# Attention of a Perceiver block: where the weights are turned, which of them are multiplied in fp32, and how far ahead the scores run

## The reference

```python
# 128 queries; 2048 context rows and the 128 latents as keys and values; DM 512
# 32 query heads of 128, 4 key/value heads, 8 query heads to each
q = (latents @ Wq).reshape(b, q_len, 4, 8, 128)
k = (hidden_states @ Wk).reshape(b, kv_len, 4, 128)      # kv_len 2176
v = (hidden_states @ Wv).reshape(b, kv_len, 4, 128)
scores = einsum('bqhgd,bkhd->bhgqk', q, k) * 128 ** -0.5
attn = softmax(scores)
out = einsum('bhgqk,bkhd->bqhgd', attn, v)
return out.reshape(b, q_len, 4096) @ Wo
```

## Time and profile before

| | |
|---|---|
| time, median of 3 runs | 661.22 us (659.51 to 661.26) |
| profiled execution | 660.41 us; span of its instructions 657.9 us |
| busy | PE 638.9 us (97%), PEld 546.6 (83%), DVE 451.4 (69%), ACT 362.3 (55%), POOL 203.9 (31%) |
| granted TensorE clock | 1.00 |
| DMA | 104.80 MB, mean 159 GB/s |
| attention loop | from about 119 us to 388 us of the span |

### The profile page before, as it was taken

One profiled execution on the slowest core, in us unless ns is written; L12 is line 12 of the kernel. 1 busy time (PEld: TensorE's weight loads), 2 busy tenths in 40 slices (PEclk: granted clock), 3 DMA queues, 4 the chain that ended last, 5 costly groups with the idle time before them and its releaser, 6 DMA issues.

```text
span 657.9 us, 12479 instructions
## 1 busy us (share of the span) xinstructions
PE 638.9 (97%) x4212; PEld 546.6 (83%) x4212; DVE 451.4 (69%) x1056; ACT 362.3 (55%) x711; POOL 203.9 (31%) x150
## 2 busy tenths in 40 slices
PE   7999999999999999999999999998999999999998
PEld 6888888898899989998999879987788797797473
DVE  3533143787788878787888665979975856758873
ACT  3413115777787778767877744767354444447210
POOL 0000000644674478447755454003320220200000
PEclk9999999999999999999999999999999999999999
DMA  7611002226254442625242656674657658597600
GB/s 254 273 64 62 4 0 69 78 69 196 73 153 121 135 137 73 195 67 193 60 130 67 229 236 166 246 281 151 237 214 269 249 201 298 212 350 294 250 1 16
DMA packets 27224, 104.80 MB, mean 159 GB/s; under 512 B 7424, under 2 KB 7808, under 8 KB 17584
## 3 DMA queue, kind: packets, MB, share of 16 engines
q1 hardware_dynamic: 26608, 103.23, 45.9%
q10 hardware_dynamic: 576, 1.05, 0.5%
HBM read 86.30 MB, written 0.26 MB: 132 GB/s over the span
## 4 chain that ended last, share of the span: by engine, by line
PE 86%; DVE 4%; POOL 4%; ACT 3%; issue 1%; DMA 1%; SPq 0%; ACTq 0%; DVEq 0%
PE ps L1467 19%; PE ps L1225 14%; PE ps L1226 14%; PE ps L1227 14%; PE ps L1507 8%; PE ps L1358 4%; PE ps L1302 3%; POOL pt_lo L430 3%; PE ps L1496 2%; PE ps L1617 2%; PE ps L1580 1%; DVE acc L1056 1%; DMA ring<-wk_dram 1%; POOL k_lo L430 1%; PE ps L1487 1%
## 5 line engine op out<-in xcount | busy, mean ns | idle before, releaser
L1467 PEld LDWEIGHTS ps<-norm_t,ring 128*128 128x128 f32 x1152 | 131.5, 192 | 4.8 <-issue 4.1
L1467 PE MATMUL ps<-norm_t,ring 128*128 128x128 f32 x1152 | 133.1, 276 | 0.0
L1056 DVE SCALAR_TENSOR_TENSOR acc<-raw,cw,acc 128x127 f32<-128x127 f32 (+2 forms) x240 | 85.9, 432 | 23.1 <-ACT acc L710 22.2
L430 POOL TENSOR_TENSOR pt_lo<-far_t,pt_hi 128x512 fp32r<-128x512 f32 (+1 forms) x75 | 87.3, 1183 | 37.9 <-ACT pt_hi L524 37.7
L1225 PE MATMUL ps<-pt_hi,v_hi 128*128 128x256 f32 x272 | 84.6, 311 | 3.0 <-POOL pt_lo L430 2.7
L524 ACT ACTIVATE pt_hi<-ps 128x512 fp32r<-128x512 f32 (+1 forms) x69 | 41.0, 596 | 67.1 <-PE ps L1358 67.0
L1227 PE MATMUL ps<-pt_lo,v_hi 128*128 128x256 f32 x272 | 76.6, 282 | 0.0
L1226 PE MATMUL ps<-pt_hi,v_lo 128*128 128x256 f32 x272 | 76.5, 281 | 0.0
L915 DVE TENSOR_SCALAR_CACHE_REDUCE prob_near<-ps 128x512 f32<-128x512 f32 x64 | 44.2, 691 | 24.4 <-PE ps L1227 22.6
L817 DVE TENSOR_TENSOR pt_lo<-ps,pt_hi 128x512 fp32r<-128x512 f32 (+1 forms) x69 | 47.4, 688 | 18.9 <-ACT pt_hi L524 17.6
L499 POOL TENSOR_SCALAR_AFFINE_SELECT at_hi<-a_hi 128x2048 fp32r<-128x2048 f32 x8 | 17.0, 2130 | 136.6 <-PE ps L1479 125.5
(11 more groups left out here) (205 smaller groups left out, 1311.0 us busy)
## 6 DMA issues: line engine op xcount, KB each, us to landing
ring<-w_in_dram SPq DMA_DIRECT2D x36, 1024.0 KB, 4.9
far_t<-blocks_t SPq DMA_DIRECT2D x240, 72.0 KB, 2.0
ring<-w_out_dram SPq DMA_DIRECT2D x16, 1024.0 KB, 4.9
ring<-wq_dram SPq DMA_DIRECT2D x8, 1024.0 KB, 5.1
ring<-wo_dram SPq DMA_DIRECT2D x8, 1024.0 KB, 6.9
w_sb<-w_dram SPq DMA_DIRECT2D x4, 896.0 KB, 9.1
ring<-ctx_t_dram SPq DMA_DIRECT2D x3, 1024.0 KB, 6.8
ring<-w_dram SPq DMA_DIRECT2D x3, 1024.0 KB, 8.6
```

The source lines that it names most:

```text
L430: sub = lambda dst, a, hi: pool.tensor_tensor(dst, a, hi, ALU.subtract)
L1056: ins = nc.vector.scalar_tensor_tensor(a[:, i, back:], r[:, i, 0:T - back], cw[:, bass.ds(tile + i, 1), 3 - back:4 - back].rearrange("p a ...
L1467: ins = mm(ps[:, bank, t * T:t * T + T], w[:, t, c, :], norm_t[:, c, :], start=(c == 0), stop=(c == NC - 1))
```

## The change

Only tiles 0 and 1 are still turned on PE, for every pair. Tiles 2 to 16 are turned on DVE in place (`p_far`, which replaces `prob_far` and `blocks_t`; two buffers now, one of them over ring slots 2 and 3), and moved by 16 DMAs of 32 partitions by 3840 B (2304 B before). Tiles 13 to 16 are multiplied in plain fp32 from `far_t` and `v_all` and need no split; the other values are split as before. The five score chunks have 256, 512, 512, 512 and 384 keys, and lie in PSUM as three pieces (256, 1024, 896 keys) in pairs of banks; DVE copies and ACT takes exp by piece. Step n makes the scores of pair n+2 (chunks 1 to 9) and chunk 0 of pair n+3, and the queries of pair n+3. Wq and Wo come in halves of 0.5 MB, one for each pair. The last two steps, 14 and 15, have their lo halves made by DVE; the last pair's moves are issued half on SP, half on ACT. The unchanged rest of the kernel begins with the norm behind the last output.

```diff
-PIECES = ((0, 512), (512, 1024), (1024, 1536), (1536, 2176))
+EDGES = (0, 256, 768, 1280, 1792, 2176)
+NEAR = 256
+PIECES = ((0, 256), (256, 1280), (1280, 2176))
+PIECE_OF = (0, 1, 1, 2, 2)
+FP32_TILES = {1: (13, 14), 2: (15, 16)}
+V_TILES = 13
+V_PARTS = ((0, 2), (2, 8), (8, 13))
+FAR_UNITS = UNITS - 3
+SCORES_LEAD = {1: (2,)}
+SCORES_AT = {0: (1,), 2: (3, 4), 3: (5, 6), 4: (7, 8), 5: (9,)}
...
+def tiles_of(u):
+    if u == 0:
+        return 0, 1
+    if u in FP32_TILES:
+        return FP32_TILES[u]
+    return tuple(t for t in (2 * u - 4, 2 * u - 3) if t < V_TILES)
...
@ SP
+            for n in range(LAST_PAIR):
+                if n + 4 <= LAST_PAIR:
+                    wq_load(n + 4)
+                moves(n + 1)
+                wo_load(n + 1)
...
+            sp.wait_ge(moved[0], MOVED * PAIRS_ALL // 2)
...
@ POOL: one pass of its loop
+                far_split(n, 3)
+                far_split(n, 4)
+                if n:
+                    wo_split(n - 1)
+                far_split(n, 5)
...
+                far_split(n, 6)
...
+                far_split(n, 7)
...
+                far_split(n, 8)
...
+            wo_split(LAST_PAIR - 2)
+            wo_split(LAST_PAIR - 1)
+            wo_split(LAST_PAIR, last_wo_lo, last_wo_hi)
@ ACT: attn_step(n, kv, p)
+                if not begin:
+                    act.wait_ge(pv_ps, 9 * n)
+                    act.wait_ge(wo_ps, 2 * n - 2)
+                    o_split(1 - b)
+                if not (isinstance(n, int) and n == LAST_PAIR):
+                    soft_exp(n + 1, 1 - b, 1, 0)
+                act.wait_ge(pv_ps, 9 * n + 1)
+                act.wait_ge(moved[b], MOVED * (2 * kv + p // 2 + 1))
+                far_split(b, 3)
+                far_split(b, 4)
+                far_split(b, 5)
...
+                if isinstance(n, int) and n == LAST_PAIR - 1:
+                    act.wait_ge(turned, 2 * LAST_PAIR + 2)
+                    act.wait_ge(pfl_ok, FAR_UNITS * (LAST_PAIR - 1))
+                    far_moves(act, LAST_PAIR, range(2, 4))
+                if not begin:
+                    wo_split(n - 1, 2 * kv + (p - 1) // 2, (p - 1) % 2)
+                if isinstance(n, int) and n == LAST_PAIR:
+                    wo_split(n, 2 * kv + 1, 1, last_wo_hi)
+                act.wait_ge(pv_ps, 9 * n + 4)
+                far_split(b, 6)
+                if not tail:
+                    soft_exp(n + 2, b, 0, 1)
...
+                act.wait_ge(pv_ps, 9 * n + 5)
+                far_split(b, 7)
+                if not tail:
+                    soft_exp(n + 2, b, 0, 2)
+                    soft_exp(n + 2, b, 0, 0)
...
+                act.wait_ge(pv_ps, 9 * n + 6)
+                far_split(b, 8)
...
+                    soft_exp(n + 2, b, 1, 1)
+                if ask:
+                    q_split(n + 3, 1 - b, 6 + (1 - b))
+                if not (isinstance(n, int) and n == LAST_PAIR):
+                    act.wait_ge(pv_ps, 9 * n + 7)
+                    near_split(n + 1)
...
+                    soft_exp(n + 2, b, 1, 2)
@ DVE: turn_far and attn_step(n, kv, p)
+                blocks = p_far[b][:, :, :, h, :]
+                nc.vector.transpose(blocks, blocks).then_inc(turned, 1)
...
+                if not end:
+                    turn_far(n + 1, 1 - b, 1)
+                if not tail:
+                    scores_out(n + 2, b, 0, 1, sent)
+                if not (isinstance(n, int) and n < 1):
+                    o_split(n - 1, 1 - b)
+                if not (isinstance(n, int) and n < 2):
+                    add_heads(n - 2, b, 1)
+                invert(n, b)
+                if tail:
+                    for u in range(3, 6):
+                        far_split(n, u)
+                else:
+                    scores_out(n + 2, b, 0, 2, sent)
+                    scores_out(n + 2, b, 1, 0)
+                if not (isinstance(n, int) and n < 1):
+                    add_heads(n - 1, 1 - b, 0)
+                if tail:
+                    for u in range(6, 9):
+                        far_split(n, u)
+                else:
+                    scores_out(n + 2, b, 1, 1, sent)
+                    scores_out(n + 2, b, 1, 2, sent)
+                    turn_far(n + 2, b, 0)
+                if ask:
+                    q_split(n + 3, 1 - b, 6 + (1 - b))
+                if not end:
+                    near_split(n + 1)
+                if ask:
+                    scores_out(n + 3, 1 - b, 0, 0)
@ PE: scores wait for the piece two before; attn_step(n, kv, p)
+                if opens and not (isinstance(m, int) and m == 0 and 3 * h + piece < 2):
+                    pe.wait_ge(s_ev, 6 * m + 3 * h + piece - 1)
...
+                for u in range(UNITS):
+                    if u == 7 and not end:
+                        transposes(n + 1, 1 - b)
+                    if not tail:
+                        more_scores(SCORES_LEAD.get(u, ()))
+                    values(n, kv, b, u, p == 0)
+                    if u == (3 if end else 4) and not begin:
+                        output(n - 1, 0)
+                    if not tail:
+                        more_scores(SCORES_AT.get(u, ()))
+                    if u == (6 if end else 7) and not begin:
+                        output(n - 1, 1)
+                    if u == 6 and ask:
+                        if not begin:
+                            pe.wait_ge(ol_ok, n)
+                        queries(n + 3, 2 * kv + (p + 3) // 2, (p + 3) % 2, 6 + (1 - b))
+                    if u == 8 and ask:
+                        pe.wait_ge(ql_ok, n + 4)
+                        if p == 1:
+                            pe.wait_ge(kl_ok, NCHUNK * (kv + 1) + 1)
+                        scores(n + 3, 1 - b, 0)
...
@ PE: ahead of step 0
-            for c in range(4):
+            for c in range(10):
                 scores(1, 1, c)
             pe.wait_ge(v_ev, 17)
+            queries(2, 1, 0, 6)
+            transposes(0, 0)
+            pe.wait_ge(ql_ok, 3)
+            scores(2, 0, 0)
```

More of the change, by code:

```diff
@@ L114, in build @@
         for s in range(4):
+            if s == 2:
+                with ExitStack() as same_place:
+                    p_far0 = sbuf(same_place, "prob_far0", [P, 4, FAR_T, 2, 32])
             add_slot(ctx, s)
@@ L244, in build @@
         x_in = sem("x_in")
+        wq_in, wo_in = [sem(f"wq_in{i}") for i in range(2)], [sem(f"wo_in{i}") for i in range(2)]
         const_in = sem("const_in")
@@ L257, in build @@
         t_ps, pth_ok, ptl_ok, pv_ps = sem("t_ps"), sem("pth_ok"), sem("ptl_ok"), sem("pv_ps")
-        turned, moved, pfl_ok = sem("turned"), sem("moved"), sem("pfl_ok")
+        turned, pfl_ok = sem("turned"), sem("pfl_ok")
+        moved = [sem(f"moved{b}") for b in range(2)]
         sum_ok, inv_ok, oh_ok, ol_ok = sem("sum_ok"), sem("inv_ok"), sem("oh_ok"), sem("ol_ok")
@@ L299, in out_chunk, with piece_banks, piece_ps, piece_prob @@
             return step_chunk(g, 4 + i)
-        def prob(b, h, lo, hi):
-            return near[b][:, h, lo:hi] if lo < NEAR else far[:, h, lo - NEAR:hi - NEAR]
-        def far_unit(b, u, w):
-            at = 2 * (2 * u - 2 * PE_UNITS)
+        def piece_banks(h, i):
+            return 2 * ((3 * h + i) % 2)
+        def piece_ps(h, i):
+            lo, hi = PIECES[i]
+            at = piece_banks(h, i)
+            flat = ps[:, at:at + 2, :].rearrange("p a n -> p (a n)")[:, 0:hi - lo]
+            return flat if i == 0 else flat.rearrange("p (t j k) -> p t j k", j=4, k=32)
+        def piece_prob(b, h, i):
+            if i == 0:
+                return near[b][:, h, :]
+            lo, hi = ((e - NEAR) // P for e in PIECES[i])
+            return p_far[b][:, :, lo:hi, h, :].rearrange("p j t k -> p t j k")
+        def far_unit(b, u):
+            at, w = 2 * (tiles_of(u)[0] - 2), len(tiles_of(u))
             return far_t[b][:].rearrange("p i t h q -> p i (t h) q")[:, :, at:at + 2 * w, :]
-        def unit_of(tile, w):
+        def unit_of(tile, u):
+            w = len(tiles_of(u))
             return tile[:, 0:w, :].rearrange("p w (h i q) -> p i (w h) q", h=2, i=4)
+        def far_moves(engine, m, rows):
+            for i in rows:
+                for j in range(4):
+                    engine.dma_start(far_t[m % 2][32 * j:32 * j + 32, i, :, :, :],
+                                     p_far[m % 2][32 * i:32 * i + 32, j, :, :, :]).then_inc(moved[m % 2], 16)
+        def wq_home(m):
+            slot = 2 if isinstance(m, int) and m < 2 else 0
+            return ring[slot]
+        def half(tile, m):
+            return tile[:, (m % 2) * 2 * DM:(m % 2 + 1) * 2 * DM]
         block = ctx.enter_context(nc.Block())
@@ new lines, in attn_step @@
+                sent = 2 * kv + p // 2 + 1
+                tail = isinstance(n, int) and n >= LAST_PAIR - 1
+                end = isinstance(n, int) and n == LAST_PAIR
+                ask = not (isinstance(n, int) and n > LAST_PAIR - 3)
+                if not end:
[4 more added lines that the diff above has]
```

(20 more changed lines are left out.)

519 lines of the change are left out of this document (216 added, 303 removed).

## The result

The changed kernel takes 655.48 us (median of 7 runs, 653.73 to 657.10) against 661.26 us (7 runs, 659.51 to 661.43): a ratio of 0.992, with a 95% interval of 0.991 to 0.993, so 5.8 us faster. The prediction was 655.5, from -15.5 us in steps 0 to 13, +7.3 ahead of them and +2.6 behind. The profiled execution took 655.37 us, its span is 653.6.

A forecast was written before the change was run, and what follows sets the result against it. PE's own work was taken to bound the attention loop. -15.5 us in steps 0 to 13, +7.3 ahead of them and +2.6 in the tail sum to -5.6, for 655.5 us; range 645 to 667.

The forecast's parts named there:

- PE sets the pace, and the fewer transposes are the gain: Attention loop: PE's own work bounds it; one transpose unit for four makes each step's transposes 1.3 us cheaper.
- The rival of the slow turns: DVE's two in-place turns a step take longer than 2.18 us each; at 3.1 us the kernel takes 667; chance 0.15.
- The fp32 tiles: Values in each step: four plain fp32 tiles at 0.44 us and 0.08 for the switch, 0.4 dearer than before.
- The wait at chunk 6: Each step: PE's chunk 6 waits about 0.3 us for DVE's copy of piece 2; 0.45 with the rest, 5.9 in all.
- Steps 0 to 13: The steady attention loop on PE: 228.6 us, 15.5 less than 244.1.
- the sign of being right: Attention loop: steps of 16.4 to 16.6 us would show the forecast right.
- The end of step 13: Step 13 has no queries, so DVE's near lo at 15.7 comes after PE is done at 14.3: +1.4 us.
- Ahead of the loop: Before step 0: it starts at 126.4, not 119.08, +7.3 us: 5.7 of work moved there, some 3 of waits.
- The tail: Steps 14 and 15 to the last output: Wo queues behind ACT's eight issues; 28.2 us against 25.6, +2.6.
- What lies behind the last output keeps its work: The kernel behind the attention's last output: its work is unchanged, so no term was given to it.
- The port: Step 15: DVE's two-input lo and POOL's Wo split exclude each other; unit 6 waits 0.8 us more, left out of the sum.

The follow-up runs named there:

- tr4: The changed kernel with the four near transposes of each pair on PE done four times over; 674.39 us.
- fp32_off: The changed kernel with the four plain fp32 tiles of steps 0 to 14 replaced by split products of the same size on other operands; 651.95 us.
- c6_late: The changed kernel with score chunk 6 moved on PE from behind unit 3 to behind the output at unit 4; 651.67 us.
- o_late: The changed kernel with DVE splitting o after the copies of pieces 2 and 3, not ahead of them, in steps 1 to 13; 655.01 us.
- fill: The changed kernel with 24 unused identity matmuls on PE where it waits ahead of the output in step 14; 654.93 us.
- wo_first: The changed kernel with ACT making Wo's hi before it issues its eight moves in step 14, not after; 650.73 us.
- c6_wofirst: The changed kernel with the changes of c6_late and wo_first together; 647.36 us.

## Why the prediction was right, step by step

- **PE sets the pace, and the fewer transposes are the gain.** Right, and shown: `tr4` gives back 95% of the work it adds. Each turn is 2.17 us, predicted 2.18; copies 1.20, 1.09 and 0.42, predicted 1.23, 1.10 and 0.42. The rival of the slow turns is out.
- **The fp32 tiles.** The term was too dear: 1.53 + 0.19 = 1.72 us instead of 1.84. Taking half of the row of 512 columns was sound, 0.19 us a record of 256 columns for 0.22; the slow start behind them was taken too small. `fp32_off` shows that they cost steps 0 to 13 2.3 us against split products that lie ready; what splitting the tiles would cost ACT and POOL wasn't measured.
- **The wait at chunk 6.** Right in place and size: predicted about 0.3 us in every step, 0.45 with the rest; measured a gap of 0.27 (once 0.39) and 0.10 of slow start. `c6_late` got 3.8 us back by the medians, 4.6 by the traces without a fall of the clock, of the 5.9 that the sum had for it and the rest. The prediction laid DVE's queue beside PE's and got the copy to start at 5.4 us by both; what holds the copy is the piece, and what counts behind it is the copy's length and the handoffs, not what is queued on DVE ahead of it, as `o_late` showed against me.
- **Steps 0 to 13.** 226.4 us for 228.6. The pitch of a step is 16.31 (16.06 + 0.45 = 16.51 predicted, and 16.4 to 16.6 was the sign of being right, so this sign was missed): 0.12 of the 0.20 is the fp32 term, and 0.07 is the wait, 0.38 for 0.45. The end of step 13, +1.4 predicted, is the wait of 1.13 at 352.34.
- **Ahead of the loop.** +6.9 for +7.3, with waits from the cause that was named, DVE's wide copies and turn: PE waits 1.56 us for DVE's q lo, which is queued behind them, ahead of step 0, where the prediction had named near lo.
- **The tail.** The mechanism was right to half a microsecond (Wo behind eight issues, PE's output at 11.2 us), the sum was not: 30.3 us for 28.2. Step 14 took 18.1 us for 16.6, step 15 with the last output 12.15 for 11.6. The term that was mis-sized is the one that priced PE's work behind the wait at the pitches of step 13: PE came back at half the clock, and `fill` gives 1.4 us for that, nearly all of step 14's 1.5. What step 15 is over is about as much as the port took there (below). `fill` and `wo_first` both show that the fall is tied to the wait: without it at this place, none.
- **Behind the attention.** "What lies behind the last output keeps its work" held for the work, but in the profiled run the time didn't: the last output is 6.2 us earlier, the end of the span 4.3. In this run a second fall of the clock lies behind 445 us (the window below); the kernel before has 1.00 in every window of 440 to 460, `wo_first` too, while `c6_wofirst` has it at 435, and the changed kernel's own runs differ by 3.4 us. What decides which execution has it stays open.

```profile
445.00:450.00 5.00, 4.29 (x22) 3.98 (x23) 5.00 (x11) 4.37 (x4) 0.00 (x0) 0.69 0.46 188
```

- **The port.** The 0.8 us that the prediction worked out for unit 6 of step 15 from the rule of the Trainium skill (SBUF — State Buffer) is there, as a wait of 0.52 us: DVE's lo starts at 378.23, POOL's subtraction runs to 378.80, and the three los take 2.06 us (1.62 in step 14, alone), 0.44 more. The rule was left out of the sum since no row had shown it; it belonged in.

```profile
378.23 2.06 DVE L902 TENSOR_TENSOR pt_lo<-far_t,pt_hi 128x512 fp32r<-128x512 f32 x3
...
376.39 2.41 POOL L482 TENSOR_TENSOR k_lo<-ring,k_hi 128x1024 fp32r<-128x1024 f32 x1
...
379.40 0.39 PE L1328 MATMUL ps<-pt_hi,v_hi 128*128 128x256 f32 x1 [0.52 <-DVE pt_lo L902]
```
